# Second attention of a macaron block: shift products in 32-row strips for two steps at a time, and another order of steps

## What is computed

```python
q = jnp.einsum('ntc,hdc->nhtd', x, w_q)
k = jnp.einsum('ntc,hdc->nhtd', x, w_k)
v = jnp.einsum('ntc,hdc->nhtd', x, w_v)
a = jnp.einsum('nhtd,nhsd->nhts', q, k) / jnp.sqrt(jnp.asarray(dk, x.dtype))
a = jnp.where(mask[None, None], jnp.asarray(-jnp.inf, a.dtype), a)
a = jax.nn.softmax(a, axis=-1)
y = jnp.einsum('nhts,nhsd->nthd', a, v)
return y.reshape(y.shape[0], y.shape[1], -1) @ w_o
```

## Time and profile before

| | |
|---|---|
| median of 3 runs | 766.88 us (765.96 to 769.78) |
| profiled execution, its own time | 767.49 us |
| its span, first to last instruction | 765.7 us |
| granted TensorE clock, mean of the span | 0.966 |
| TensorE busy (matmuls) | 696.4 us, 91% |
| VectorE busy | 577.0 us, 75% |
| GpSimd busy | 499.2 us, 65% |
| ScalarE busy | 445.5 us, 58% |

### The profile page before, as it was taken

The page is one execution under the profiler, slowest core; times in us unless marked ns, Lnnn a source line. Parts: engine busy times, 40 slices in busy tenths (PEclk is TensorE's granted clock), DMA queues, the critical chain, the costliest instruction groups (busy, mean ns, idle before and its releaser), DMA issues. The chain is left out here.

```text
span 765.7 us, 21921 instructions
## 1 busy us (share of the span) xinstructions
PE 696.4 (91%) x9509; PEld 413.8 (54%) x9511; DVE 577.0 (75%) x808; ACT 445.5 (58%) x536; POOL 499.2 (65%) x387
## 2 busy tenths in 40 slices
PE   2756888888889899999999999999999999999997
PEld 1523445444444454565655556556667555566774
DVE  7698897898998886778778777665676766774286
ACT  2333665988777769545655756555624565655511
POOL 6862245506854410389899999968981979999910
PEclk9856998999999999999999999999999999999999
DMA  8000000000000000001001011011101101101010
GB/s 275 8 1 2 3 2 3 2 3 3 2 3 3 2 3 3 3 3 30 3 30 30 3 29 32 4 29 30 31 3 30 30 3 30 30 6 45 12 29 29
DMA packets 13015, 15.68 MB, mean 20 GB/s; under 512 B 3000, under 2 KB 10488, under 8 KB 12920
## 3 DMA queue, kind: packets, MB, share of 16 engines
q1 hardware_dynamic: 12344, 13.96, 6.4%
q10 hardware_dynamic: 576, 0.33, 0.1%
HBM read 12.74 MB, written 1.16 MB: 18 GB/s over the span
## 5 line engine op out<-in xcount | busy, mean ns | idle before, releaser
L742 ACT ACTIVATE Pr<-ps 128x1024 f32<-128x1024 f32 (+1 forms) x258 | 237.8, 965 | 96.0 <-PE ps L1345 50.0
L1171 DVE TENSOR_REDUCE mxb<-ps 128x8 f32<-128x1024 f32 (+1 forms) x147 | 172.1, 1194 | 72.5 <-PE ps L1345 44.4
L725 POOL TENSOR_TENSOR V0s<-V0s,Pr 128x1024 f32<-128x1024 f32 x66 | 161.9, 2453 | 63.0 <-PE ps L1294 46.9
L1140 DVE TENSOR_REDUCE big<-ps 128x8 f32<-128x1024 f32 (+1 forms) x166 | 171.5, 1077 | 24.0 <-PE ps L1324 15.3
L1345 PE MATMUL ps<-big 64*128 64x128 f16 (+2 forms) x2560 | 169.0, 259 | 2.8 <-DVE mxb L1171 1.4
L1324 PE MATMUL ps<-big 32*128 32x128 f16 (+2 forms) x1280 | 102.0, 276 | 35.7 <-DVE big L1140 21.5
L1345 PEld LDWEIGHTS ps<-big 64*128 64x128 f16 x2560 | 92.1, 94 | 65.3 <-issue 22.1
L1324 PEld LDWEIGHTS ps<-big 32*128 32x128 f16 x1280 | 42.7, 95 | 108.6 <-ACT Pr L742 36.1
L1294 PE MATMUL ps<-Pr,V1s 128*64 128x256 f32 (+2 forms) x704 | 92.9, 404 | 0.4 <-ACT Pr L742 0.4
L725 POOL TENSOR_TENSOR acts<-acts,Pr 128x1024 f32<-128x1024 f32 x30 | 73.8, 2461 | 10.7 <-PE ps L1294 5.6
L1264 PE MATMUL ps<-Pr,V0s 128*18 128x128 f32 (+2 forms) x1280 | 80.3, 378 | 0.3 <-ACT Pr L749 0.3
(11 more groups left out here) (261 smaller groups left out, 1034.8 us busy)
## 6 DMA issues: line engine op xcount, KB each, us to landing
rec_b<-scratch_dram SPq DMA_DIRECT2D x28, 256.0 KB, 3.9
X<-in_x_dram SPq DMA_DIRECT2D x2, 256.0 KB, 3.5
big<-in_pick_rows_dram SPq DMA_DIRECT2D x2, 256.0 KB, 3.7
X<-in_x_dram SPq DMA_DIRECT2D x1, 512.0 KB, 6.3
rec_b<-in_w_q_dram SPq DMA_DIRECT2D x1, 512.0 KB, 6.1
XT<-in_w_k_dram SPq DMA_DIRECT2D x1, 512.0 KB, 6.9
XT<-in_w_v_dram SPq DMA_DIRECT2D x1, 512.0 KB, 8.0
wo_s<-in_w_o_dram SPq DMA_DIRECT2D x1, 512.0 KB, 9.2
```

The costliest lines, as they stand in the source:

```text
L725: g.tensor_tensor(dst, dst, src, ALU.add).then_inc(summed, 1)
L742: ins = a.activation(dst[:, part], src, func, scale=scale)
L1140: ins = v.tensor_reduce(maxima_of(mall[:, r, 2 * u:2 * u + 2][:, part], i), block_view(src, i), AX.X, ALU.max, negate=True)
L1171: ins = v.tensor_reduce(maxima_of(mxb[:, r][:, part], arg), block_view(src, arg), AX.X, ALU.max, negate=True)
```

## The change

1. Each part of the shift rows is written twice by the SP queue, four DMAs for a pair where two were: the high and the low part of a head now lie in rows 0 and 1 of a strip of 32 rows, head 0 in strips 0 and 2, head 1 in strips 1 and 3.
2. Where two *exp* steps that are not diagonal stand next to each other in `PLAN` (41 places), the first one waits for the banks of both, and `shift_slots` issues the shift products of both steps first, each head and step in a strip of its own. The three products of the one and then of the other step follow. An *exp* step that stands alone keeps its shift product of 64 rows, behind its three, with a table `shr64` that picks one copy (30 steps); one of pair 0 takes the strips alone.
3. `shr64` is loaded by one DMA of the SP queue into the memory of the first attention's values, when those are no longer read; TensorE waits for it at pair 1.
4. The diagonal cuts are 60, 60 and 8 columns wide in place of 62, 62 and 4, as four rows of 64 are held by the shift in place of two.
5. `ORDER` is another string from its first line to its last. The kinds and numbers of steps are the same.

```diff
-CUTS = (0, 62), (62, 124), (124, 128)
+CUTS = (0, 60), (60, 120), (120, 128)
...
-    "mhhewmmQKQtVVMegeeMweMeweMeweMeweMeweMeweMeweeMgeewTKKQwwMMgEEEMWWMEEMWMMhMEEMEEMQKhTWhhWWWMEhMhhWWM"
+    "mhhewmmKQQtVVMegeeMweMeweMeweMeweMeweMeweMeweeMgeewTKKQwwMMgEEEMWMEMWMMVhMEEMEEMETWMMQhKWWWWhMEhMhWW"
...
+def paired_shifts():
+    firsts, seconds = set(), set()
+    for n in range(1, len(PLAN)):
+        both = (PLAN[n - 1], PLAN[n])
+        if n - 1 not in seconds and all(kind == "exp" and arg not in DIAGONAL for kind, _, arg, _ in both):
+            firsts.add(n - 1)
+            seconds.add(n)
+    return firsts, seconds
...
+        shr64 = V0s[:, 4 * S:4 * S + P // 2].bitcast(BF16)
...
-                        sp.dma_start(SQ[key % 2][32 * w:P:D1, :], sht[w][:, key % 2]).then_inc(shift_set, 16)
+                        for twin in range(2):
+                            at = SQ[key % 2][D1 * twin + w:D1 * (twin + 1):HR, :]
+                            sp.dma_start(at, sht[w][:, key % 2]).then_inc(shift_set, 16)
+                if kind == "exp" and (key, arg) == (0, 0):
+                    sp.wait_ge(pv0, CH * G)
+                    sp.dma_start(shr64.bitcast(U16), own_rows).then_inc(own_in, 16)
...
+            def shift_slots(steps):
+                rows_in = sorted((len(E_PLACED[PLAN[n][2]]), n, twin) for twin, n in enumerate(steps))
+                for q in range(rows_in[-1][0]):
+                    for count, n, twin in rows_in:
+                        if q < count:
+                            _, a0, a1, off = E_PLACED[PLAN[n][2]][q]
+                            for h in range(2):
+                                rows = slice(HR * (2 * twin + h), HR * (2 * twin + h + 1))
+                                te.matmul(slot_of(n)[h][:, off:off + a1 - a0], shr[rows], SQ[PLAN[n][1] % 2][rows, a0:a1],
+                                                start=q == 0, stop=False)
...
-                wait_for_banks(n)
+                if n not in SECONDS:
+                    wait_for_banks(n)
...
-                        pe.wait_ge(shift_set, 32 * (key + 1))
+                        pe.wait_ge(shift_set, 64 * (key + 1))
+                        if key == 1:
+                            pe.wait_ge(own_in, 16)
                     diagonal = arg in DIAGONAL
+                    alone = not diagonal and key > 0 and n not in FIRSTS | SECONDS
+                    if n in FIRSTS:
+                        wait_for_banks(n + 1)
+                        shift_slots((n, n + 1))
+                    elif not (diagonal or alone or n in SECONDS):
+                        shift_slots((n,))
                     ins = pair_scores(slot, E_PLACED[arg], lambda t, a0, a1: [
                         (KH[r][:, tile(t)], QH[r][:, a0:a1]), (KH[r][:, tile(t)], QL[r][:, a0:a1]),
-                        (KL[r][:, tile(t)], QH[r][:, a0:a1])] + [(shr, SQ[key % 2][:, a0:a1])] * (not diagonal), diagonal)
+                        (KL[r][:, tile(t)], QH[r][:, a0:a1])] + [(shr64, SQ[key % 2][:, a0:a1])] * alone, diagonal, diagonal or alone)
```

More of the change, by code:

```diff
@@ L216 @@
 ORDER = (
[L217 to L220, removed]
-    "mhhewmmQKQtVVMegeeMweMeweMeweMeweMeweMeweMeweeMgeewTKKQwwMMgEEEMWWMEEMWMMhMEEMEEMQKhTWhhWWWMEhMhhWWM"
[L222 to L227, removed]
+    "hhammmmmmmmmmmmmmammmmmmmtamemmemmeeheemwhmemwmeewmmewmhewmemhemewemetwmemwmeheewemehhhwemewmamegeem"
+    "wmemweemhmwmmhmemmewemewmewmhhmhthmemhhmehmemwemmwmegeemhmhhwmewmemeameweemeweemwmteewmememwmemwemem"
+    "heewemwememaemwmeewemmhwmewmetmhwmegememehmwmemwemgehmmhmamhheeweemhwheemwmemwehemweemmwemwemtmhwmea"
+    "mmhehemwemweemewehhhemwemewemewemewemmmheetwmehhhhhhhwhhhehhmwmegmehememwmehhewemewemewemewmemwememw"
+    "mmhewmmKQQtVVMegeeMweMeweMeweMeweMeweMeweMeweeMgeewTKKQwwMMgEEEMWMEMWMMVhMEEMEEMETWMMQhKWWWWhMEhMhWW"
+    "hSMhEEMWMEEMEEMEMWTMEMWhVhKQWWWWWhMEMWMhEEMWhWMEEMTSMEEEMWWWMEEMWMMQhVKhhWWWMEEMEEEMMWWMMhEWEMSThhVh"
+    "WWWMEEMWhWWMEEEMhhVKhQWWMETSEhhMMWWMEEEEMWWWWWMMQVKhEhEEhMWWWWMEEMMWTSMEEMWWMEEMWWMEEhMMWWWQKVSTMEEE"
+    "EEMWWWEMMWWMEMWMEEQKWWMEEMEEMSTWWWWMEEEMWWWMEEEEMWWMEMWMMVQKVSTEMEEMWWWMEMWWWMEEEEEEEWWWMMKQOOMMOSTM"
+    "WMEMWWMMVKQOMEMhhWWWMEEMEEEMMWWMMMWWWTSMEEEEMVhQKhWhhhWWWMEEMEEEMMWWWWMSTMEMWMEEEMhKVQhWWWWMEEMEEMEM"
+    "WWMSTEMMWWWWMEEhEMWWWMEEEMKhQWWWSTMEEEhMWWWWMEEEhVVWWMhEEMWWMhEMWMEEMESTEEWWWWWWEEEEWWWWXEEOXEEXEXFW"
+    "hFFOFLWWWWXLLFXOFOLFFLFLLLL"
 )
@@ L242 @@
 ADD_FAST = ((2, 1),)
+def paired_shifts():
[6 more added lines that the diff above has]
+    return firsts, seconds
+FIRSTS, SECONDS = paired_shifts()
 def filled(*key):
@@ L292, in macaron_block_kernel @@
 def macaron_block_kernel(nc, x, w_kqv, w_o0, w_int, w_scale, bias, w_q, w_k, w_v, w_o1, w_gate, w_up,
-                         w_down, ident, rope_cos, rope_sin, cut_q, cut_k, pick, cut_q0, cut_k0, pick0, shift_rows, pick_rows,
+                         w_down, ident, rope_cos, rope_sin, cut_q, cut_k, pick, cut_q0, cut_k0, pick0, shift_rows, own_rows, pick_rows,
                          scratch, out):
@@ L448, in macaron_block_kernel @@
         pv1, acc1_saved, summed = sem("pv1"), sem("acc1_saved"), sem("summed")
-        mx_ready, shift_set = sem("mx_ready"), sem("shift_set")
+        mx_ready, shift_set, own_in = sem("mx_ready"), sem("shift_set"), sem("own_in")
         sums_in, rec_done, rec_out, rec_in, normed = (sem("sums_in"), sem("rec_done"), sem("rec_out"), sem("rec_in"),
@@ L1336, in shift_and_cut, with pair_scores @@
                 return ins
-            def pair_scores(slot, pieces, products, goes_on):
+            def pair_scores(slot, pieces, products, goes_on, begins=True):
                 for q, (t, a0, a1, off) in enumerate(pieces):
@@ L1345, in pair_scores @@
                             ins = te.matmul(slot[h][:, off:off + a1 - a0], still[rows], moving[rows],
-                                            start=q == 0 and k == 0,
+                                            start=begins and q == 0 and k == 0,
                                             stop=not goes_on and q == len(pieces) - 1 and k == len(made) - 1)
                 return ins
+            def shift_slots(steps):
[8 more added lines that the diff above has]
+                                                start=q == 0, stop=False)
             def add_up(p, slot):
@@ L1615, in _constants @@
     lane = np.arange(P)[None, None, :]
-    free = np.array([r % D1 - 1 - (r % D1 > 32) for r in range(P)])[:, None]
-    held = np.arange(P)[:, None] % 32 == 0
+    free = np.array([r % D1 - 2 - 2 * (r % D1 > 33) for r in range(P)])[:, None]
+    held = np.arange(P)[:, None] % HR < 2
+    own = held & (np.arange(P)[:, None] % D1 // HR == np.arange(P)[:, None] // D1)
     width = CUTS[0][1]
-    cut_k = np.stack([np.where(held, np.float32(SHIFT_TOP), np.where(lane[0] > c0 + free, np.float32(-1e30), np.float32(0)))
+    cut_k = np.stack([np.where(own, np.float32(SHIFT_TOP), np.where(~held & (lane[0] > c0 + free), np.float32(-1e30), np.float32(0)))
                       for c0, _ in CUTS], axis=1)
@@ L1633, in _constants @@
         "pick0": bits(np.arange(P)[:, None] % HR == np.arange(HR)[None, :]),
-        "shift_rows": bits(np.where(np.arange(P)[:, None] % 32 == 0, np.float32(SHIFT_TOP), np.float32(0))
-                           * np.ones((1, P), np.float32)),
+        "shift_rows": bits(np.where(held, np.float32(SHIFT_TOP), np.float32(0)) * np.ones((1, P), np.float32)),
+        "own_rows": bits(np.where(own, np.float32(SHIFT_TOP), np.float32(0)) * np.ones((1, P), np.float32)),
         "pick_rows": pick_rows,
```

## The result

The changed kernel takes 791.57 us (median of four runs, 789.74 to 793.48) where the kernel before takes 766.94 (four runs): 1.0315 times as long, interval 1.0277 to 1.0353. It is slower, as forecast, but by 24.6 us where 7.3 were forecast, and outside the range. The profiled execution is 790.84 us, its span 789.0 against 765.7.

The account below looks back on a forecast made before the run. TensorE was taken to bound 310 to 720 us, every column and wait paid in full; -8.8 + 7.6 + 7.5 + 1.0 = +7.3 us on 767.5 gave 774.8, median forecast 774.2 us, range 761 to 784.

Parts of the forecast that it names:

- Columns: TensorE, second attention's exp pairs: one shift pass in four strips replaces two at 41 pairs, 8.8 us less.
- The 0.05 that was kept as an end: Four strips' extra time over one pass, 0.05 us at 41 pairs, 2.0 us; taken as 0, kept as 0 to 2.0.
- Changes of rows: TensorE switching between 64-row and 32-row matmuls: 78 more changes at 0.097 us, 7.6 us more.
- The wait for two pairs of banks: Ahead of paired exp steps, TensorE waits for both steps' banks: 7.5 us more, ends 2 and 15.3.
- Two things take from it: Discounts on the 15.3 us pair wait: 5.9 less ordinary waiting in the new order, then a share of 0.59.
- a share of 0.59: Old order's 12.8 us of idle weight loads before scores against 21.7 counted; scaled the pair wait to 5.5.
- The order: New step order on TensorE: ordinary waits counted as 15.8 us against 21.7 in the old, 5.9 less.
- The doubled DMAs: SP queue's last shift row issues 1.2 us later, so first exp steps wait: 1.0 us more, 0 to 2.7.
- The first attention: Stretch before 310 us, newly ordered, seven more row changes: no gain or loss, 0, with 4 us either way.
- the order that pays: Rival: fewer ordinary waits, pair waits mostly hidden, better first attention; -5.7 us, about 761; chance 0.18.
- the cancelling: Rival: a wait ahead of a pair lets readers catch up and next waits vanish; 767; chance 0.19.
- The one that has strips not side by side: Rival: strips of two steps run behind one another, a pair keeps two passes; 783; chance 0.07.

## Why the prediction was right in its direction and wrong in its size

**Columns: right.** The strips' group lies behind one pass where there were two. From the first strip to the first product behind it are 0.331 us in the mean of 42 places: 0.215 for a pass, 0.097 for the change, 0.02 left. Runs of two strips, in the kernel with strips at each step, take 0.32, so four cost 0.01 more than two. The 0.05 that was kept as an end was not there. The Trainium skill (TensorE: Matmul & The Clock Gate, part 3, measured speedup) has four strips at 3.07 times one. The trace does not bear it out here: 0.02 us at 42 places is 0.8 us, where the prediction's estimate from that figure is 2.7.

**Changes of rows: right.** 0.097 us was the price from the earlier trace rows, and in the changed kernel a change from 64 to 32 rows and one back take about that again. Between first turn and last weigh step its trace has 224 where there were 146: 78 more, as counted.

**The wait for two pairs of banks: the mechanism right, the size wrong.** This is a step that failed, and the largest. The count, bank by bank, gave 18.3 us, less 3.0 for the changes under the waits, 15.3. The trace has 16.1 us before the strips. What failed are the discounts behind the sentence "Two things take from it", which made 7.5 of 15.3. The first took off 5.9 us of "less ordinary waiting" in the new order: with the code before, that order has no more than 0.5 us less of it at the score products (2.0 for 2.5), and 15.1 us of weight-load waits where the old has 12.8. The second took a share of 0.59 from the weight loads' idle time. That is no price of a wait on TensorE: the products stood idle for 2.5 of those 12.8 us, and an estimate from the distances of their starts gives no more than 4. So the share says how far the count overstates ordinary waits (by more than was thought), and nothing of the waits for two steps' banks, which mostly came to their count: 16.1 us for 15.3 in the new order, and, with nothing else changed in the old one, 12.5 where the count without discounts has 38.0 - 21.7 = 16.3. Why the one count holds so much better than the other was not taken apart. With the count as it stood, -8.8 + 7.6 + 15.3 = 14.1 us for the pairs; the runs have 17.1 in the new order, 15.1 of them behind the first turn, and 14.1, for 39 pairs, in the old. 15.3 was kept as the far end; it should have been the value.

**The order: missed.** This is the second step that failed. The order was costed by counting readers of banks, as if the other engines were always there in time. It cost 6.8 us with the code before. The tail is 4.3 longer there (3.3 in the changed kernel); in it the output step waits 3.0 us for GpSimd, ScalarE and VectorE, and the low clock behind it costs some 1.7. No term of the sum stood for the tail, though the change names the whole string.

**The doubled DMAs: inside their range, and less than the value taken.** 1.0 was forecast, between 0 and 2.7. In the changed kernel TensorE waits 0.2 us for the shift rows, in the old program 0.5. The 0.75 that was measured with the table and the cut widths holds the 14 changes of pair 0 too and is within the noise. In the order of before the wait is 1.2 us longer.

**The first attention: right.** The stretch did not move by more than 0.3 us in TensorE's and VectorE's busy time, and the second attention starts 1.0 us later, at 306.1 us, in the middle of the 304.1 to 308.9 of the new order's executions.

Together: 6.8 for the order, 0.75 for rows and table, 17.1 for the pairs, 24.6. The three are steps from kernel to kernel, so they add up by construction, and each is known to a few us. Of the 17.3 us that the forecast fell short, the pairs' waits are 8.6 (16.1 for 7.5) and the order is 6.8. Of the rivals the order that pays is refuted (773.71 with the old code) and so is the cancelling (the waits of the earlier trace rows are still there, and longer). The one that has strips not side by side came nearest in time, by chance: its mechanism is not there.

## What to carry to other kernels

A step that asks for two slots of a three-slot ring must have the reader done one step earlier: count what the reader still needs at that place, and discount it only by a row that shows what hides it (here 16.1 us came of 15.3 counted in one order, 12.5 of 16.3 in the other). Idle time of weight loads is not idle time of the products: price a wait by the second. A pass saved by narrower row strips is worth one change of rows each way (0.215 against twice 0.097 us here), so by these numbers strips would pay only where they stand among other strips, which no run here tried. When a whole order of steps changes, follow the chains through the other engines up to the tail, where little work is left to fill a wait.

## What the runs showed that had not been expected

A single wait of TensorE late in the program was paid twice: after 3.0 us without work in the tail the granted clock stood at 0.50, which is 1.2 GHz, for 3.4 us, though it had been at 1.00 since 230 us, and the same 36 matmuls took 3.48 us for 2.17. It was seen in the changed kernel, in the one with only the new order, in the two others that have the new tail and a wait of 3.0 us there (without pairs, and with the strips between the products), and, at another place, behind the wait of 2.22 us in the one with the step moved. The 16.1 us of short waits before the strips, none over 1.4 us, left the clock at 1.00 from 310 to 720 us. How long the wait was does not settle it. With strips at each step the same place in the tail waits 2.23 us, and the clock behind it is 1.00 (the timeline, and the busy times behind it):

```profile
760.67 0.63 PE L1625 MATMUL ps<-id_s,D 128*128 128x128 f32 x4 [2.23 <-DVE last_rec L1227]
```

```profile
761.00:765.00 4.00, 4.00 (x59) 3.35 (x58) 3.83 (x14) 0.60 (x1) 0.00 (x0) 1.00 0.01 4
```

And behind the wait for the shift rows at pair 1, of 1.7 us without pairs and 1.8 with them (both in the order of before), the clock stayed at 1.00 in the first profile and was 0.86 in the mean of the twelve microseconds from 338 us in the second. What decides it no run here shows.
